# Second experts: all routed units' token weights by way of DRAM, two banks for the up product, and another order of steps

## The reference, cut to what matters

```python
def _L1_ffn_ref(x, gate_w, wg, wu, wd, swg, swu, swd):
    HIDDEN, N_EXPERTS, TOP_K, INTER, N_SHARED = 128, 8, 2, 176, 2
    xf = x.reshape(-1, H)
    scores = softmax(xf @ gate_w.T)
    topw, topi = top_k(scores, TOP_K)
    topw = topw / (topw.sum(axis=-1, keepdims=True) + 1e-20)
    wdense = zeros((T, N_EXPERTS)).at[arange(T)[:, None], topi].set(topw)
    hg = einsum('th,ehi->eti', xf, wg)
    hu = einsum('th,ehi->eti', xf, wu)
    eo = einsum('eti,eih->eth', silu(hg) * hu, wd)
    y = einsum('te,eth->th', wdense, eo)
    shared = silu(xf @ swg) * (xf @ swu) @ swd
    return (y + shared).reshape(B, S, H)
```

## Time and profile before

| quantity | value |
|---|---|
| median of 3 runs | 487.06 us (486.44 to 488.05) |
| span of the profiled execution | 484.9 us |
| PE busy | 413.4 us, 85% of the span |
| DVE busy | 333.5 us, 69% |
| ACT busy | 293.4 us, 61%, of it 42 table loads 53.9 us |
| POOL busy | 125.2 us, 26% |
| DMA | 46.62 MB, mean 96 GB/s |

### The profile page before, as it was taken

How to read it: one execution, slowest core, us unless ns; L and a number is a source line. 1 busy time by engine, 2 the same in 40 slices (tenths; PEclk the granted TensorE clock), 3 DMA queues, 4 the chain that set the end, 5 groups by cost and what they waited for, 6 DMA issues and landing times.

```text
span 484.9 us, 5925 instructions
## 1 busy us (share of the span) xinstructions
PE 413.4 (85%) x2035; PEld 202.0 (42%) x2035; DVE 333.5 (69%) x616; ACT 293.4 (61%) x508; POOL 125.2 (26%) x129
## 2 busy tenths in 40 slices
PE   5968988888889999999977875557889899999995
PEld 2443533443345554434343221232666544544442
DVE  1386567789969953562799999899977543564454
ACT  4865697526245678889576896456347575652125
POOL 1100000000382029007966667745000200000000
PEclk9999999958789999999997996667989999999999
DMA  8950000564181000005008857979500000501401
GB/s 280 341 153 30 1 2 0 170 90 150 50 191 25 2 4 3 2 15 161 0 18 239 211 168 214 213 206 278 230 0 1 1 0 17 159 1 53 123 0 43
DMA packets 26109, 46.62 MB, mean 96 GB/s; under 512 B 7397, under 2 KB 12742, under 8 KB 24918
## 3 DMA queue, kind: packets, MB, share of 16 engines
q1 hardware_dynamic: 25972, 46.15, 33.6%
q10 hardware_dynamic: 108, 0.10, 0.1%
HBM read 41.13 MB, written 5.01 MB: 95 GB/s over the span
## 4 chain that ended last, share of the span: by engine, by line
PE 58%; DVE 19%; ACT 12%; issue 5%; POOL 3%; DMA 2%; SPq 1%; DVEq 0%; ACTq 0%
ACT AR L1207 7%; DVE AR L1553 7%; PE PS L924 7%; PE PS L956 6%; PE PS L929 5%; PE PS L852 4%; PE PS L838 4%; PE PS L821 3%; ACT L1203 3%; PE PS L688 3%; PE PS L1007 2%; DVE stats L1562 2%; DVE AR L1559 2%; POOL AR L2195 2%; DVE AR L1878 2%
## 5 line engine op out<-in xcount | busy, mean ns | idle before, releaser
L1207 ACT ACTIVATE AR<-PS 128x512 f32<-128x512 f32 (+3 forms) x187 | 98.9, 563 | 103.3 <-PE PS L924 49.5
L1553 DVE TENSOR_TENSOR AR<-PS,AR 128x512 f32<-128x512 f32 (+1 forms) x104 | 69.1, 675 | 49.6 <-PE PS L929 30.4
L2195 POOL TENSOR_TENSOR AR<-AR 128x512 f32<-128x512 f32 (+2 forms) x48 | 52.5, 1101 | 137.3 <-DVE AR L1553 106.7
L1207 ACT ACTIVATE AR<-AR 128x256 f32<-128x256 f32 (+3 forms) x110 | 46.7, 463 | 44.3 <-DVE AR L1553 28.0
L1203 ACT ACT_TABLE_LOAD x42 | 53.9, 1283 | 0.8
L1562 DVE TENSOR_REDUCE stats<-PS 128x1 f32<-128x512 f32 (+4 forms) x88 | 43.6, 521 | 10.3 <-PE PS L762 4.3
L1878 DVE TENSOR_TENSOR_SCAN AR<-PS,AR 128x512 f32<-128x512 f32 x32 | 38.8, 1212 | 1.3 <-ACT PS L1207 0.7
L821 PE MATMUL PS<-RR 97*128 97x512 bf16 (+3 forms) x128 | 34.1, 344 | 4.2 <-DVE stats L1562 3.3
L688 PE MATMUL PS<-AR,W_sq 128*128 128x256 f32 x88 | 27.3, 424 | 10.8 <-ACT AR L1207 6.3
L1553 DVE TENSOR_TENSOR AR<-AR 128x512 f32<-128x512 f32 (+2 forms) x48 | 32.3, 689 | 3.9 <-ACT AR L1207 2.6
L1207 ACT ACTIVATE AR<-PS,W_vec 128x256 f32<-128x256 f32 (+1 forms) x46 | 24.2, 545 | 12.6 <-PE PS L688 4.3
(11 more groups left out here) (241 smaller groups left out, 712.8 us busy)
## 6 DMA issues: line engine op xcount, KB each, us to landing
AR<-scan SPq DMA_DIRECT2D x64, 256.0 KB, 3.9
RR<-in_ffn SPq DMA_DIRECT2D x1, 2688.0 KB, 11.1
RR<-in_ones SPq DMA_DIRECT2D x2, 832.0 KB
RR<-in_ones SPq DMA_DIRECT2D x2, 784.0 KB
RA<-in_moe SPq DMA_DIRECT2D x1, 1539.5 KB, 6.2
AR<-weights SPq DMA_DIRECT2D x6, 256.0 KB, 4.8
W_mla<-in_mla SPq DMA_DIRECT2D x1, 1504.0 KB, 15.9
W_late<-in_late SPq DMA_DIRECT2D x1, 1076.0 KB, 11.5
```

What stands on the lines that cost most here:

```text
L1207: nc.scalar.activation(out_, in_, func, bias=bias, scale=scale).then_inc(*done("act", *step))
L1553: nc.vector.tensor_tensor(out_, a, b_, op).then_inc(*done("dve", *step))
L2195: nc.gpsimd.tensor_tensor(out_, a, b_, op).then_inc(*done("pool", *step))
```

## The change

Four things are changed.

1. `FROM1` goes. All 11 routed units' weights are read from DRAM (18 reads for a sequence in place of 13), into other buffers. `sel1` and its load are gone, and with them three selection products, the bf16 transposes, the ACT copy `wt1`, and on DVE the split into parts (4 small steps a sequence).
2. `ewf` is now four fp32 transposes of `wn` itself, after the up product of unit 2, in bank 2.
3. The up product alternates between banks 1 and 2: unit k waits for the DVE product of unit k-2. Unit 3, which takes over bank 2 from `ewf`, waits for `ewc`.
4. `TURNS` and `TABLES` are new throughout: on all engines the lanes are interleaved another way, and ACT has 45 table loads in place of 42.

```diff
-FROM1 = SH1 + 3
...
         if p == "e" and k == 2:
+            out += ["ewf"]
...
-        "mx", "ms", "su", "iv", "pr1", *_PICK1[:5], *_E1[0], *_PICK1[5:9], *_E1[1], *_PICK1[9:],
+        "mx", "ms", "su", "iv", "pr1", *_PICK1[:5], *_E1[0], *_PICK1[5:9], *_E1[1], *_PICK1[9:10],
...
-        "a4 b1 a2 w1 a2 w1 a1 w1 b1 a3 w1 a1 w2 a13 b1 a2 b3 a1 b2 a3 b1 a4 b1 a1 b1 a1 b6 a1 b1 a1 b1 a1 b3 "
+        "a3 w1 a1 w1 a1 w1 a5 b1 w3 a6 b1 a12 b4 a1 b2 a1 w1 a6 b2 a1 b1 a1 b6 a2 b4 a2 b1 a14 b2 a1 b6 a2 w1 a2 "
...
-    "2:log 11:gelu 12:log 14:gelu 17:exp 26:log 40:gelu 47:log 51:gelu 52:exp 64:log 91:gelu 100:log "
+    "2:log 11:gelu 14:exp 26:log 40:gelu 47:log 51:gelu 53:exp 65:log 92:gelu 96:sin 101:log 105:sin 107:log "
...
         def unit_weights(b, k):
-            return A(b, 8 + k - FROM1)
+            return A(b, (1, 2, 0, 8, 9, 10, 11, 12, 13, 14, 15)[k - SH1])
+
+        def up_bank(b, p, k):
+            return own(b, (1, 2)[k % 2] if p == "e" else 1)
...
-            load("sel1", tiles["sel1"])
             for b in range(B):
                 sp.wait_ge(*after("act", b, "ewc"))
                 sp.dma_start(weights_dram[b], A(b, 3)[0:E1, :]).then_inc(weights_out[b], 16)
                 sp.wait_ge(weights_out[b], 16)
-                for k in range(FROM1, UB1):
+                for k in range(SH1, UB1):
...
-                        if k:
+                        if p == "e":
+                            if k == 1:
+                                pe.wait_ge(*after("dve", b, "ms"))
+                            elif k == 3:
+                                pe.wait_ge(*after("act", b, "ewc"))
+                            elif k:
+                                pe.wait_ge(*after("dve", b, f"{d}u{k - 2}"))
+                        elif k:
                             pe.wait_ge(*after("dve", b, f"{d}u{k - 1}"))
-                        mm(own(b, 1), w(group, "u", 128 * k, 128), x, start=True, stop=True)\
+                        mm(up_bank(b, p, k), w(group, "u", 128 * k, 128), x, start=True, stop=True)\
...
+                        if p == "e" and k == 2:
+                            pe.wait_ge(*after("dve", b, "eu1"))
+                            pe.wait_ge(*after("dve", b, "wn1"))
+                            for t in range(NT):
+                                last = tr(own(b, 2)[0:E1, 128 * t:128 * t + 128], routing(b, 784 + E1 * t, E1), w("sq", "id"))
+                            last.then_inc(*done("pe", b, "ewf"))
...
-                            if p == "e":
-                                mm(own(b, 2)[0:E1, :], w(sel, "s")[0:WROWS, 0:E1 * I1:I1], wT[b][:, :], start=True, stop=True)\
-                                    .then_inc(*done("pe", b, "ewf"))
...
                 if k >= shared:
-                    apart = p == "e" and k >= FROM1
+                    apart = p == "e"
                     if apart:
                         dve.wait_ge(weights_in[b, k], 16 * len(pieces(k)))
```

More of the change, by code:

```diff
@@ L109, in unit_steps @@
         out += [f"{p}g{k}", f"{p}u{k}"]
-        if k == shared:
-            out += [f"{p}wt"] + ["ewf"] * (p == "e")
-        if k >= shared and (p != "e" or k < FROM1):
+        if p == "e" and k == 2:
+            out += ["ewf"]
+        if p != "e" and k == shared:
+            out += [f"{p}wt"]
+        if p != "e" and k >= shared:
             out += [f"{p}w{k}"]
@@ L190 @@
         "u0", "u1", "u2", "u3", *_ln("lno"), *_ln("ln5"), "rt1",
-        *[x for k in _K for x in [f"el{k}"] + ["wt1", "ewc"] * (k == SH1)], *_ln("ln6")],
+        *[x for k in _K for x in [f"el{k}"] + ["ewc"] * (k == 2)], *_ln("ln6")],
     "dve": [
@@ L351, in build @@
         weights_in = {(b, k): ctx.enter_context(nc.semaphore(f"weights_in{b}_{k}")) for b in range(B)
-                      for k in range(FROM1, UB1)}
+                      for k in range(SH1, UB1)}
         kernel_dram = nc.dram_tensor("kernel_rows", (D, T), F32, kind="Internal").ap()
@@ L930, in units @@
                             .then_inc(*done("pe", b, f"{p}u{k}"))
                         yield
-                        if k == shared:
-                            turn_weights(b, f"{p}wt", wl, 3 * e, 2)
-                            yield
-                            pe.wait_ge(*after("act", b, wt))
-                            pe.wait_ge(loads[sel], 16)
-                            if p == "e":
-                                mm(own(b, 2)[0:E1, :], w(sel, "s")[0:WROWS, 0:E1 * I1:I1], wT[b][:, :], start=True, stop=True)\
-                                    .then_inc(*done("pe", b, "ewf"))
+                        if p == "e" and k == 2:
+                            pe.wait_ge(*after("dve", b, "eu1"))
[3 more added lines that the diff above has]
+                            last.then_inc(*done("pe", b, "ewf"))
+                            yield
@@ L940, in units @@
+                        if p != "e" and k >= shared:
+                            if k == shared:
+                                turn_weights(b, f"{p}wt", wl, 3 * e, 2)
                                 yield
-                                pe.wait_ge(*after("act", b, "ewc"))
-                        elif shared < k and (p != "e" or k < FROM1):
-                            pe.wait_ge(*after("dve", b, f"{d}w{k - 1}"))
-                        if k >= shared and (p != "e" or k < FROM1):
+                                pe.wait_ge(*after("act", b, wt))
+                                pe.wait_ge(loads[sel], 16)
+                            else:
+                                pe.wait_ge(*after("dve", b, f"{d}w{k - 1}"))
@@ L1383, in gates @@
                     yield
-                    if k == shared:
+                    if p == "e" and k == 2:
+                        act.wait_ge(*after("pe", b, "ewf"))
+                        f(A(b, 3)[0:E1, :], own(b, 2)[0:E1, :], ACT.Copy, (b, "ewc"))
+                        yield
+                    if p != "e" and k == shared:
                         act.wait_ge(*after("pe", b, f"{p}wt"))
@@ L1387, in gates @@
                         yield
-                        if p == "e":
-                            act.wait_ge(*after("pe", b, "ewf"))
-                            f(A(b, 3)[0:E1, :], own(b, 2)[0:E1, :], ACT.Copy, (b, "ewc"))
-                            yield
             def first_experts(b):
```

16 lines of the change are left out of this document (8 added, 8 removed), and 43 rows, old and new, of tables (TABLES, TURNS).

## The result

The changed kernel takes 492.54 us against 487.56 us for the kernel before (medians of 4 runs each), a ratio of 1.0108 (95% interval 1.0083 to 1.0133). The prediction of 485.0 us, range 481.0 to 490.3, was wrong in sign. The profiled span is 489.7 us, 4.8 us longer than before.

The account below looks back on a forecast made before the run. It took PE as the bound from 145 to 245 and 387 to 478 us, DVE from 245 to 345 us. Its terms, -0.9 + 0 - 0.7 - 0.8 + 1.3 - 1.0 = -2.1 us, gave 485.0 us, range 481.0 to 490.3.

Parts of the forecast that it names:

- A: Second experts: PE work removed, transposes and a DRAM wait added, net -0.9 us, from -2.0 to +3.3.
- B: Start: a's first residual earlier, `kl` and `ql` later, neither carried far: 0 us, from -2.5 to +1.4.
- C: Maxima: five DVE steps of lane w leave, mostly covered by PE: -0.7 us, from -2.9 to 0.
- D: b's routing before a's scan: two DVE steps freed from POOL, half counted: -0.8 us, from -1.65 to +1.65.
- E: Four more ACT table loads up to a's last scan exponential, one on the path: +1.3 us, from 0 to +5.1.
- the sign of E: Expected evidence: 45 loads, and the time from `a.dl` to a's last scan row longer by about a load.
- Rival 2: Scan, 260 to 290 us: ACT becomes the bound through added table loads; 490.6 us, chance 0.15.
- F: a's Fourier block: DVE steps leave the path from convolution to MLP, half of 2.01 us counted: -1.0 us, from -2.0 to 0.
- Rival 3: Attention: PE idles near 142 us, another half-clock stretch after 145 us costs 4.3 us; 489.3 us, chance 0.13.
- The prediction's sign of being wrong: Any of: scan stretch longer by over one load, clock below 1 after 145 us, reads landing later than 5.5 us.

Follow-up runs that it names:

- second trace of the changed kernel: The changed kernel, unaltered, run again beside later experiments on one chip: 493.45 us, ratio 1.0154 to the kernel before.
- the new front: New order up to the start of b's first maxima; with new experts and the old order behind it, 487.58 us, ratio 0.9991 to the kernel before.
- all three: Changed kernel with five DVE table steps later, b's router exponential behind a's norm, POOL waiting for b's split: 486.99 us, ratio 1.0023 to the kernel before.
- norm first: Changed kernel with b's router exponential on ACT moved behind a's norm after the first experts: 490.86 us, ratio 1.0059 to the kernel before.

## Why the prediction was wrong, by its own steps

**A, the second experts: right.** -0.9 us predicted; from `b.X5` to `b.X6` it is 62.49 us after 63.48, so -1.0, and -1.3 in the kernel that has this edit alone. The parts hold as well: PE's wait in a is 1.20 us (1.4 predicted), none is seen in b (0.1), the four transposes take 0.60 us, the write's issue to the first read 413.44 - 411.95 = 1.49 us. With 36 reads the landings are closer together than the earlier trace rows: 3.4, 4.5 and 5.1 us.

**B, the start: right in the sum.** a's first residual came 2.73 us earlier (at 55.99 us, not near 38) and `ql` 3.35 us later, and neither is shown to have been carried: with `kl` and `ql` early the time is the same within its interval.

**C, the maxima: the size by luck.** `a.mx7.E` ends 1.8 us earlier in the changed kernel, but in the kernel that has the old order in this stretch it ends 1.3 us earlier too (138.36), by a lead that it has from the start (`a.X1` 1.1 us earlier). Within the maxima, from `a.mx0.E` to `a.mx7.E`, it is 31.67 us after 32.54, so -0.9 where -0.7 was predicted. The reason given isn't there: DVE is busy 28.61 us in this stretch after 28.62, so it was not relieved, while the granted clock was 0.88 after 0.79.

**D, POOL beside DVE: the steps were freed, but the scan didn't wait for them.** The two routing steps of b take 0.19 and 0.18 us now. In their place another, of 128x196, is stretched beside POOL's next product (0.34 us before):

```profile
258.62 1.43 DVE L1558 TENSOR_TENSOR stats<-stats 128x196 f32<-128x196 f32 x1
```

So "it may press other steps" was right, and half was a fair guess. But the two steps stand behind `a.dl` (the earlier trace rows begin at 255.22 us, `a.dl` ended at 253.16), so they couldn't delay a's scan. What did get shorter is `a.X3` to `a.dl`, 4.39 us after 6.19, and that largely since steps of lane w left it: they and the ones ahead of them went among a's first experts, which made place 2. In the four kernels that move them back it is 5.92. And the step that came under POOL instead, b's split at 179 us, lies in the PE-bound stretch and got no price; it costs 0 to 2.6 us, by execution.

**E, the table loads: not shown to cost.** There are 45 loads, as said. From `a.dl` to `a.hc15` it is 53.61 us after 52.36, a load more, as the sign of E asked; but the second trace of the changed kernel has 51.34. From a's first scan step `a.sc0` to `a.hc15` the ten traces with the new order there have 40.8 to 44.3 us, mean 42.2, the four with the old one 40.7 to 42.0, mean 41.4: 0.8 us apart, inside the spread. The predicted +1.3 us isn't confirmed and isn't excluded. Rival 2 falls: the scan isn't where the time went.

**F, the Fourier block: right.** From `b.X4`, the residual ahead of it, to `a.lnf.x` it is 15.79 us after 16.82, -1.0 as predicted. The ten traces with the new order there have 15.0 to 15.8 us, the four with the old one 15.7 to 16.8.

**The step that failed is one that isn't in the sum.** From 145 to 247 us the prediction read the earlier trace rows as PE-bound, and since the work there is the same, it gave the new order no term. But the bound holds only while nothing that PE waits for comes later. From `a.mx7.E` to `a.de` the stretch is longer by 8.3 us: 2.0 for b's first maxima and the half clock behind them, 3.1 at the end of a's attention, -1.0 in b's, 2.7 for the table steps ahead of a ready expert product, 1.4 for the exponential ahead of a ready norm. Each of these stands in the order: a product moved up to the step that feeds it, or a step that waits for another engine put ahead of one that is ready.

**Rival 3 had the mechanism and one place in four.** PE waits for the copies through DRAM at 140.34 us and the clock falls at 141.4; its price for the fall was 4.3 us, and measured it is about 1.5. The prediction's sign of being wrong, a clock below 1 after 145 us, came as well: 0.99 from 145 to 245 us, by the fall at 243.8. Its time, 489.3 us, was too low because it looked at one wait only. Rival 2's 490.6 us is nearer to the result, but by a mechanism that isn't there. The clock isn't lower over the whole span (mean 0.937 after 0.927); some of the half clock now lies where PE sets the end.

**Open** remain what brings on the slower course of some executions of the new front, with half clock from 133 to 150 us, and 1.1 us of the row to `b.su23`, which no wait in the trace accounts for. Giving `a.yt` its cover back by an edit of its own wasn't tried; that the old order as a whole has 41.6 us there in each trace that has it, and the new one never less than 44.66, is all that is shown.

## What to carry to other kernels

An engine runs its program in order: a step put ahead of a ready one costs its own length and also its wait, and a product moved close behind the step that feeds it loses its cover. "PE-bound" in a window doesn't make a reorder there free; go through every step that PE waits for in the stretch and ask what now stands ahead of it, and what runs beside it on POOL. To compare two orders, cut the traces where the same steps are done in both: the undisturbed ones repeated to 0.1 us here, where the times spread by 9 us.

## What the runs showed of the hardware

POOL's 128x512 fp32 products stretch DVE's smallest steps by the largest share: 0.18 us becomes 0.93 to 1.09 us each, while steps of 128x1024 go from 0.75 to 1.52 and from 1.23 to 1.95 us (DVE of the kernel "all three", where POOL isn't beside them), by 0.7 to 0.8 us as well:

```profile
244.64 0.75 DVE L1561 TENSOR_SCALAR RR<-RR,W_vec 128x1024 f32<-128x1024 f32 x1
245.42 1.23 DVE L1564 SCALAR_TENSOR_TENSOR RR<-RR 128x1024 f32<-128x1024 f32 x1
```

It is an amount per step and not a share, so a chain of short steps suffers most. Steps that take an input from PSUM kept their time beside POOL: in the changed kernel a 128x128 product took 0.29 us at 184.23 us, with POOL busy, as at 176.78 without it, and the scan's 32 steps 1.212 us at the median after 1.211. A product of POOL takes 14.07 / 12 = 1.17 us in the row of place 1, and each slow step lost most of one. The Trainium skill, page "SBUF — State Buffer", section "Who interferes with whom", states that a DVE step with two SBUF inputs, or in a two-port mode, contends with a POOL step that reads SBUF, and that whichever of the two issues first has the shared ports for its whole instruction while the other waits; the trace agrees with 0.7 to 0.9 us lost per step.

The granted clock fell to half (1.2 of 2.4 GHz) behind the waits of PE of 1.63, 1.80 and 1.83 us shown above, and stayed at full behind those of 0.88, 1.19 and 1.40 us, but also behind the one of 1.81 us at place 2 (the kernel "norm first"). So the length of the wait alone doesn't tell. One edit of order can so cost 2 us in one execution and next to nothing in another, as the first row of the table of stretches has it for the changed kernel (18.46 and 16.69 us).
